# Output product of one tile moved between two prefix sums, and row statistics moved along four queues, in an attention and FFN kernel

## The reference, cut to what matters

```
x = x + attn(layernorm(x))          # x: 4 batches of 512 rows, 512 columns, float32
x = x + ffn(layernorm(x))

attn(x):  q  = x @ W_q.T,  kv = x @ W_kv.T          # 16 heads of 32
          qf, kvf = fft over each head, each divided by its norm
          kvf = cumsum(kvf, over the rows of the batch)
          values = real(ifft(qf * kvf))
          return values @ W_o.T
ffn(x):   gate = silu((x @ f8(gate_w)) * gate_scale),  up = (x @ f8(up_w)) * up_scale
          return ((gate * up) @ f8(down_w)) * down_scale      # 1536 inner columns
```

## Time and profile before

| | us |
|---|---|
| time, median of 3 runs | 418.65 |
| lowest and highest of the 3 | 418.07, 419.58 |
| the profiled execution's own time | 418.57 |
| its span, first to last instruction | 416.8 |
| TensorE busy | 408.6 |
| VectorE busy | 298.1 |
| ScalarE busy | 193.4 |
| GpSimd busy | 109.2 |

### The profile page before, as it was taken

How to read it: one execution, slowest core, us unless ns; L and a number is a source line. 1 busy time by engine, 2 the same in 40 slices (tenths; PEclk the granted TensorE clock), 3 DMA queues, 4 the chain that set the end, 5 groups by cost and what they waited for, 6 DMA issues and landing times.

```text
span 416.8 us, 5552 instructions
## 1 busy us (share of the span) xinstructions
PE 408.6 (98%) x1921; PEld 205.8 (49%) x1921; DVE 298.1 (72%) x516; ACT 193.4 (46%) x324; POOL 109.2 (26%) x114
## 2 busy tenths in 40 slices
PE   8999999999999999999999999999999999999995
PEld 4744454445555554454555555454444444445442
DVE  5998998999989699997984972167855853422235
ACT  3687656586736245445242563345533341132220
POOL 0133641015254137043541013032462001300003
PEclk9999999999999999999999999999999999999999
DMA  8997547600281153232112015401112041200002
GB/s 260 269 253 240 167 113 165 165 0 2 42 238 51 26 77 70 58 125 77 28 26 50 2 25 102 76 36 66 26 26 52 0 76 26 101 2 0 2 0 101
DMA packets 57691, 33.55 MB, mean 81 GB/s; under 512 B 49472, under 2 KB 50112, under 8 KB 57536
## 3 DMA queue, kind: packets, MB, share of 16 engines
q1 hardware_dynamic: 57232, 32.93, 31.0%
q10 hardware_dynamic: 432, 0.28, 0.2%
HBM read 17.44 MB, written 4.19 MB: 52 GB/s over the span
## 4 chain that ended last, share of the span: by engine, by line
PE 86%; DVE 4%; POOL 2%; DMA 2%; ACT 2%; issue 1%; SPq 1%; POOLq 0%; ACTq 0%; DVEq 0%
PE bu L477 19%; PE bg L477 18%; PE bd L504 17%; PE ba L376 14%; PE ba L422 8%; PE bd L376 3%; PE bd L344 2%; DMA h<-x_dram 1%; PE bd L422 1%; PE ba L395 1%; DMA qk<-qk 1%; PE bd L362 1%; PE bu L422 1%; POOL h L1674 1%; DVE y L1143 1%
## 5 line engine op out<-in xcount | busy, mean ns | idle before, releaser
L477 PE MATMUL bu<-hT,gu 128*128 128x512 f16 x384 | 90.7, 379 | 0.0
L477 PE MATMUL bg<-hT,gu 128*128 128x512 f16 x376 | 89.0, 379 | 0.3 <-ACT sl L757 0.3
L1258 DVE SCALAR_TENSOR_TENSOR ff<-bu,us,sl 128x512 f32<-128x512 f32 x47 | 35.2, 748 | 53.9 <-PE bu L477 50.5
L757 ACT ACTIVATE sl<-bg,gs 128x512 f32<-128x512 f32 x48 | 32.9, 686 | 78.1 <-PE bg L477 77.0
L376 PE MATMUL ba<-wf,xT 128*128 128x512 f16 x288 | 63.2, 379 | 0.0
L477 PEld LDWEIGHTS bu<-hT,gu 128*128 128x128 f16 x384 | 37.5, 98 | 45.5 <-DVE ff L1258 0.6
L477 PEld LDWEIGHTS bg<-hT,gu 128*128 128x128 f16 x376 | 35.6, 98 | 43.6 <-issue 4.1
L504 PE MATMUL bd<-dw,fu 128*128 128x512 f32 x192 | 51.1, 411 | 0.1
L1674 POOL TENSOR_TENSOR h<-ff,h 128x512 f32<-128x512 f32 x14 | 17.5, 1269 | 121.3 <-DVE ff L1300 121.3
L376 PEld LDWEIGHTS ba<-wf,xT 128*128 128x128 f16 x288 | 27.9, 98 | 34.1 <-issue 1.1
L1643 POOL TENSOR_TENSOR xs<-xn,xs 128x512 f16<-128x512 f32 x15 | 20.4, 1368 | 78.5 <-ACT xs L669 78.5
(11 more groups left out here) (210 smaller groups left out, 540.7 us busy)
## 6 DMA issues: line engine op xcount, KB each, us to landing
h<-x_dram SPq DMA_DIRECT2D x16, 256.0 KB, 4.1
out_dram<-h SPq DMA_DIRECT2D x14, 256.0 KB, 2.0
hT<-w_q_dram SPq DMA_DIRECT2D x4, 256.0 KB, 4.0
gu<-w_kv_dram SPq DMA_DIRECT2D x4, 256.0 KB, 4.1
hT<-gate_w_dram SPq DMA_DIRECT2D x2, 512.0 KB, 3.7
hT<-up_w_dram SPq DMA_DIRECT2D x2, 512.0 KB, 6.0
gu<-woT_dram SPq DMA_DIRECT2D x1, 1024.0 KB, 5.2
hT<-down_w_dram SPq DMA_DIRECT2D x2, 512.0 KB, 5.0
```

The costliest lines, as they stand in the source:

```text
L477: m = e.matmul(bk[:, :], gu[:, c, 4 * w + k, col:col + P], hT[:, b % 2, part, k, :], start=k == 0 and part == 0, stop=k == KT - 1 and part ...
L757: e.activation(sl[:, n % 2, :], bg[:, :], ACT.Silu, scale=gs[:, i:i + 1]).then_inc(a_silu, 1)
L1258: e.scalar_tensor_tensor(out=ff[:, n % 2, :], in0=bu[:, :], scalar=(us if b < HALF else us2)[:, i:i + 1], in1=sl[:, n % 2, :], op0=ALU.mul ...
```

## The change

No operation is added or taken away; what changes is the order, the banks that follow from it, and the order of the matmuls inside an output product. On TensorE `pe_o(0,0)` now comes straight after tile 2's prefix sum, then the transposes of tile 1, then tile 3's prefix sum. Inside `pe_o` all high-by-high products come first, then the low part of the left operand, then the low part of `wo`, and in batch 0 each group waits for its own operand. ScalarE copies `pT` before the low parts of `wo`; `act_ks(1,1)` moves behind silu 3; batch 2's root moves from behind silu 4 to behind silu 9, its first `xh` from behind `ks(1,2)` to behind silu 10. VectorE does both output additions of tiles 2 and 3 before `hT(0,0)`; the four `stats1` of batch 2 move from before `dve_f(0)` and after `dve_f(3)` to behind rounds 12 and 13 and behind `dve_o(1,0)`; root and `xn` follow. On the SP queue the four `hT` transposes of batch 0 go ahead of weight loads 7 and 8, and `sp_xT(2,0)` goes between `sp_zT(1,2)` and `sp_zT(1,3)`.

```
@@ tenancies
-    order += [("pT", 0, 0), ("tri", 0, 2), ("tri", 0, 3), ("pT", 0, 1), ("o", 0, 0), ("pT", 0, 2), ("o", 0, 1),
-              ("pT", 0, 3), ("o", 0, 2), ("o", 0, 3), ("qk", 1, 0, 0), ("qk", 1, 0, 1)]
+    order += [("pT", 0, 0), ("tri", 0, 2), ("o", 0, 0), ("pT", 0, 1), ("tri", 0, 3), ("pT", 0, 2), ("o", 0, 1),
+              ("pT", 0, 3), ("qk", 1, 0, 0), ("o", 0, 2), ("o", 0, 3), ("qk", 1, 0, 1)]
@@ pe_o
-            if b == 0:
-                e.wait_ge(a_pT, t + 1)
-                e.wait_ge(v_pT, t + 1)
-            else:
+            if b > 0:
                 e.wait_ge(d_zT[t], 32 * b)
-            if b == 0 and t == 0:
-                e.wait_ge(a_wolo, KT)
-            for j in range(KT):
-                for part_p, part_w in ((0, 0), (0, 1), (1, 0)):
+            for part_p, part_w in ((0, 0), (1, 0), (0, 1)):
+                if b == 0 and part_w == 0:
+                    e.wait_ge(v_pT if part_p else a_pT, t + 1)
+                for j in range(KT):
+                    if b == 0 and t == 0 and part_w == 1:
+                        e.wait_ge(a_wolo, j + 1)
                     m = e.matmul(ba[i][:, :], src[:, part_p, P * j:P * j + P], wo[:, part_w, j, :],
-                                 start=j == 0 and part_p == part_w, stop=j == KT - 1 and part_p == 1)
+                                 start=j == 0 and part_p == part_w, stop=j == KT - 1 and part_w == 1)
@@ tensor_program
             pe_tri(e, 0, 2)
+            pe_o(e, 0, 0)
+            pe_pT(e, 0, 1)
             pe_tri(e, 0, 3)
-            pe_pT(e, 0, 1)
-            pe_o(e, 0, 0)
             pe_o(e, 0, 1)
@@ scalar_program
+            act_pT(e, 0)
             act_wo_low(e, 0)
-            act_pT(e, 0)
...
             act_hT(e, 0, 1)
+            act_sqrt2(e, 0, [2, 3])
             act_qk(e, 1, 1, 0)
-            act_sqrt2(e, 0, [2, 3])
             act_hT(e, 0, 2)
             act_qk(e, 1, 1, 1)
+            act_hT(e, 0, 3)
             act_qk(e, 1, 2, 0)
-            act_hT(e, 0, 3)
...
-            act_ks(e, 1, 1)
             act_fu(e, 2)
             act_silu(e, 3)
+            act_ks(e, 1, 1)
             act_half(e, 9)
...
             act_silu(e, 4)
-            act_root0(e, 2, range(NT))
             act_row(e, 1, 1)
...
             act_ks(e, 1, 2)
-            act_xh(e, 2, 0)
             act_silu(e, 7)
...
             act_silu(e, 9)
+            act_root0(e, 2, range(NT))
             act_ks(e, 1, 3)
             act_half(e, 17)
             act_fu(e, 9)
             act_zh(e, 1, 2)
             act_silu(e, 10)
+            act_xh(e, 2, 0)
             act_zh(e, 1, 3)
@@ vector_program
             dve_o(e, 0, 2)
+            dve_o(e, 0, 3)
+            dve_ln2_head(e, 0, [2, 3])
+            dve_hT(e, 0, 0)
             dve_sum(e, 1, 0, 0)
-            dve_hT(e, 0, 0)
-            dve_o(e, 0, 3)
+            dve_ln2_tail(e, 0, [2, 3])
             dve_hT(e, 0, 1)
-            dve_ln2_head(e, 0, [2, 3])
-            dve_ln2_tail(e, 0, [2, 3])
             dve_hn(e, 0, 2)
...
             dve_sum(e, 1, 1, 0)
+            dve_hT(e, 0, 3)
             dve_sum(e, 1, 1, 1)
-            dve_stats1(e, 2, 0)
             dve_round(e, 4)
-            dve_hT(e, 0, 3)
             dve_sum(e, 1, 2, 0)
-            dve_stats1(e, 2, 1)
...
             dve_round(e, 6)
-            dve_stats1(e, 2, 2)
             dve_f(e, 0)
...
             dve_f(e, 3)
-            dve_stats1(e, 2, 3)
             dve_fu(e, 2)
             dve_fu(e, 3)
-            dve_root0_head(e, 2, range(NT))
             dve_round(e, 9)
-            dve_root0_tail(e, 2, range(NT))
...
             dve_scale(e, 1, 2, 0)
-            dve_xn(e, 2, 0)
             dve_f(e, 5)
             dve_round(e, 11)
             dve_fu(e, 4)
-            dve_xn(e, 2, 1)
+            dve_stats1(e, 2, 0)
             dve_round(e, 12)
...
             dve_round(e, 13)
+            dve_stats1(e, 2, 1)
             dve_f(e, 7)
...
             dve_o(e, 1, 0)
+            dve_stats1(e, 2, 2)
+            dve_stats1(e, 2, 3)
             dve_fu(e, 8)
+            dve_root0_head(e, 2, range(NT))
             dve_f(e, 9)
             dve_round(e, 15)
             dve_round(e, 16)
             dve_product(e, 1, 3)
             dve_zl(e, 1, 2)
+            dve_root0_tail(e, 2, range(NT))
+            dve_xn(e, 2, 0)
+            dve_xn(e, 2, 1)
             dve_f(e, 10)
@@ gpsimd_program
-            pool_xl(e, 2, 0)
             pool_product(e, 1, 1)
             pool_product(e, 1, 2)
             pool_ks(e, 1, 3)
             pool_product(e, 1, 3)
+            pool_xl(e, 2, 0)
@@ sync_program
             sp_x(e, 2, 2)
-            sp_weights(e, 7)
-            sp_weights(e, 8)
             sp_hT(e, 0, 0)
-            sp_x(e, 2, 3)
             sp_hT(e, 0, 1)
             sp_hT(e, 0, 2)
             sp_hT(e, 0, 3)
+            sp_weights(e, 7)
+            sp_weights(e, 8)
+            sp_x(e, 2, 3)
...
-            sp_xT(e, 2, 0)
             sp_weights(e, 17)
             sp_zT(e, 1, 1)
             sp_zT(e, 1, 2)
+            sp_xT(e, 2, 0)
             sp_zT(e, 1, 3)
```

## The result

| | before | changed |
|---|---|---|
| median of 22 runs, us | 418.81 | 420.01 |
| lowest and highest | 417.69, 419.90 | 418.72, 420.51 |
| profiled execution | 418.57 | 420.11 |
| its span | 416.8 | 418.3 |

The ratio is 1.0025, with a 95% interval from 1.0016 to 1.0034: slower, by 1.05 us, within the 0.3% that the prediction counts as no change. Forecast were 419.1 us and 0.57 us over the kernel before. The measured 420.01 us is inside the range of 8 in 10 (417.6 to 420.3) and just above the forecast's own range (418.4 to 419.7).

The account below looks back on a forecast made before the run. TensorE bounds the kernel, busy 408.6 of 416.8 us. A 1.33 us lead (0.86 + 0.47) was to turn into 0.57 us of delay through late VectorE and the SP queue: 418.57 + 0.57 = 419.1 us, own range 418.4 to 419.7, 8-in-10 range 417.6 to 420.3.

Parts of the forecast that it names:

- the ceiling: Most an order could win from TensorE's two waits ahead of 150 us: 1.52 us, 0.36% of the time.
- First wait: Before tile 1's transposes (L406), held by a GpSimd copy: output product moved ahead gains 0.86 of 1.05 us.
- the second case of rival (b): o(0,0) gets operands late, first 0.86 us not won: 419.9 to 420.0; chance 0.2 shared with the first case.
- The stretch before the first gate: From batch 1's remaining projections to the first gate: nothing lost; moving weight loads 7 and 8 behind hT transposes wins nothing.
- The narrow margin at `qk(1,2,1)`: ScalarE frees the bank at 72.1, TensorE wants it at 72.23: margin 0.1 us, where it was 0.66.
- The first case of rival (b): Chain through hT(0,0) overruns its margin at qk(1,2,1), 0.9 us over giving 420.0; chance 0.2 shared with the second case.
- Second wait: Before gate 4: silu 3 ahead of act_ks(1,1) removes the whole 0.47 us; the copy behind is late by nothing.
- the lead: TensorE's gain from both removed waits: 0.86 + 0.47 = 1.33 us ahead of the kernel before.
- The bill: VectorE, multiply of round 13 to product of tile 3: added statistics stretch 16.02 us to 18.04, ending 0.69 us later.
- Rival (c): Round 15 on VectorE is not stretched by the GpSimd copy, saving 0.6 us: total 418.5; chance 0.2.
- The SP queue collects the bill: Tile 3's transposes leave behind the x pair, land at 149.8; its output product waits from 147.9, 0.57 us net delay.
- The sum: At the end of the kernel: 0.57 us delay carried unchanged from 150 us, 418.57 + 0.57 = 419.1 us.

Follow-up runs that it names:

- e9: Changed kernel with batch 2's stats1 of tiles 1 to 3 ahead of round 13 and sp_xT(2,0) behind sp_zT(1,3): 417.38 us, ratio 0.9966 to before.
- e3: Kernel before with only sp_xT(2,0) moved between sp_zT(1,2) and sp_zT(1,3): 418.75 us, ratio 1.0005 to before.
- e4: Kernel before with only batch 2's rows moved on the four queues as in the change: 421.08 us, ratio 1.0054 to before.
- e5: Kernel before with only act_fu(2) and silu 3 put ahead of act_ks(1,1): 418.43 us, ratio 0.9993 to before.
- e11: The changed kernel itself, timed once more: 419.85 us, ratio 1.0023 to before.
- e6: Changed kernel with batch 2's rows and silu 3 put back, leaving only the edits ahead of the first gate: 418.36 us, ratio 0.9992 to before.
- e7: Changed kernel with batch 2's stats1 of tiles 1 to 3 moved ahead of round 13 on VectorE: 418.23 us, ratio 0.9986 to before.
- e8: Kernel before with only TensorE's new order, the banks, the inside of pe_o and ScalarE's earlier pT copy: 418.42 us, ratio 0.9990 to before.
- e10: Changed kernel with batch 2's rows put back on all four queues, same as e2, timed again: 418.40 us, ratio 0.9988 to before.
- e2: Changed kernel with batch 2's rows (stats1, root, xn, xh, xl, sp_xT(2,0)) put back on all four queues: 417.53 us, ratio 0.9972 to before.
- e1: Changed kernel with only sp_xT(2,0) moved back behind sp_zT(1,3) on the SP queue: 418.61 us, ratio 1.0002 to before.

## Why the prediction was right, and where it was off

**What bounds the kernel, and the ceiling.** Right as far as the runs tell. Both old waits went, and the most that a version won is e9's 1.4 us (0.34% of 419.08), just under the ceiling of 1.52. Its interval, 0.9 to 2.0 us, takes in both sides of the ceiling, so the ceiling as such was not tested.

**First wait.** The mechanism was right, the size not. I took 0.86 us from one execution. A better measure is from the start of tile 0's transposes to the start of the 72 projections. In the profile of before it is 21.39 us (65.32 less 43.93) and in the changed one 20.61. But in e3, where this part is as before, it is 21.07. The rows of TensorE in e3:

```profile
44.51 0.60 PE L406 MATMUL bu<-cst,qk 128*128 128x128 f32 x4
...
48.70 0.63 PE L406 MATMUL bd<-cst,qk 128*128 128x128 f32 x4 [0.56 <-POOL qk L1669]
...
65.58 15.70 PE L376 MATMUL ba<-wf,xT 128*128 128x512 f16 x72
```

In e4 it is 21.13 (65.00 less 43.87), in e5 21.06. With the new order e9, e11, e6, e7, e8 and e10 have 20.53 to 20.56, e2 20.68, and e1 20.93 (64.58 less 43.65): there `o(0,0)` started 0.2 us late and took 0.2 us longer, a part of the second case of rival (b). So between the two profiles the gain is 0.78 us, and the means of the four executions of the old order (21.16) and the nine of the new (20.61) are 0.55 apart. GpSimd's chain to the copy stands 0.3 us earlier relative to TensorE in e3, e4 and e5 than in the profile that I had. e6 and e8, whose times give about 0.4 us, fit this size better than 0.86.

**The stretch before the first gate.** The narrow margin at `qk(1,2,1)` held: the 72 projections are one row. The first case of rival (b) did not occur. Doubtful is that the hT transposes ahead of the weight loads win nothing: in the one trace without them (e8) TensorE's lead loses 0.42 us at the first gate. The times of e6 and e8 do not show it.

**Second wait.** Right in place: gate 4 follows without a gap in every kernel that has the silu ahead. Its size too came from one execution: 0.47 us there and 0.52 in e4, but in e3, with the same order, 0.16. The rows of TensorE in e3:

```profile
97.62 1.89 PE L477 MATMUL bu<-hT,gu 128*128 128x512 f16 x8
99.51 1.89 PE L477 MATMUL bg<-hT,gu 128*128 128x512 f16 x8
```

That the copy behind it is late by nothing held in the changed kernel, where the moved statistics let tile 0's transposes of batch 1 leave 0.8 us earlier (109.20 against 110.03). With the statistics in their old place the lead loses 0.12 and 0.26 us to their landing (e2, e10), and 1.4 in e5 with its slow landing. I had not counted this.

**The bill.** Right, shown by e7 and e9 against the changed kernel and e1. 18.04 us were forecast from the multiply to the product, 18.19 came. `fu 8` became short as assumed (0.66). Rival (c) was half right: the first part of round 15 took 0.68 us, unstretched, but its multiply, from 135.87, took 2.07 instead of 1.23, beside the GpSimd operation that the prediction calls a copy. It is the subtraction that forms the keys' low part, and its row is

```profile
135.47 1.39 POOL L1655 TENSOR_TENSOR ks<-qk,ks 128x512 f16<-128x512 f32 x1 [2.56 <-ACT ks L719]
```

The cover was not gone, it moved to the next instruction, and in e7 and e9 the multiply takes 2.07 us too. By the rule of the Trainium skill (SBUF — State Buffer, "SBUF: two separate sides"), that whoever starts first on the shared ports holds them, the trace agrees nearly: the subtraction came first, ended at 136.86, and the multiply ended 1.08 us after that, where its own length is 1.23.

**The SP queue collects the bill.** Right that it adds to it: the pair left in the forecast order and the wait appeared. But the expectation of e1 called the queue's order the only way in which the late VectorE costs, and that is wrong: with the order mended (e1) 1.5 us of VectorE's lateness remain against e9. From the issue of tile 3's pair to the output product it took 3.93 us (150.80 less 146.87), where 3.73 were summed.

**The sum.** 0.57 us was forecast, 1.05 measured, nearly twice as much. Between the two profiles, counted from tile 0's transposes, the delay is 0.94 us (106.24 less 105.30), 0.37 more than forecast. Three terms were too kind: the multiply of round 13 came 0.07 us late because the first gain was 0.78 and not 0.86, the stretch on VectorE was 0.15 longer, and the way from the split through the queue to the landing took 0.15 more. The mis-sized term beyond that is the lead: both waits of the old kernel, 1.05 and 0.47 us, were read in one execution, and in e3 they are 0.73 and 0.16. An execution of the old order with smaller waits is faster by about as much (104.71 us instead of 105.30), and the change costs more against it. The delay is 0.94 us against the one and 1.5 against the other; the 1.05 measured lies between. How often each size occurs in the 22 executions is open. Carrying the delay unchanged to the end was right: 267.4 to 267.6 us follow in every kernel.

## What to carry to other kernels

Before work moves along a queue, find the stretch where that engine has no gap and ends in a transfer that someone waits for: three short row statistics cost nothing that was seen ahead of round 13 and about 1.5 us behind it. A lead won at one wait can be spent at the next one, so look what else must come forward with it (the transposes of e8, the split of e5). A move that is harmless without a lead can cost once there is one: the x pair's place cost nothing in e3 and 0.8 us between e9 and e7. Two moves are priced by all four combinations: e1 alone looked as if VectorE's lateness cost little, because the gains hid it. And a wait sized in one execution should be sized in a second before it carries a sum.

## What the hardware showed that I had not expected

The order of the engines against each other ahead of 44 us is not the same in two executions: the start of tile 0's transposes scattered over 1.0 us (43.65 to 44.69), and a wait of the same code was 0.89 us in one execution and 0.56 to 0.63 in three others (the transposes of tile 1 in before, e3, e4, e5). The landing of one transpose took 3.6 us instead of 2.5 (e5), in a stretch where weight loads were issued behind it.
